# VectorE instead of GpSimd adds the probability blocks of a pair of heads in a transformer kernel

## The reference

```python
x = L0_attn_x                                              # (8, 512, 128)
x = x + _L0_attn_ref(_layernorm(x), Wq, Wk, Wv, g_scale)   # 16 heads of 8, cosine attention, no mask
x = x + _L0_ffn_ref(_layernorm(x), ...)                    # top-1 of 8 experts, hidden width 32
x = x + _L1_attn_ref(_layernorm(x), w_q, w_k, w_v, w_o)    # 16 heads of 64, causal
x = x + _L1_ffn_ref(_layernorm(x), ...)                    # top-2 of 8 experts, hidden width 512, norm
# the causal attention of the second layer:
a = jnp.einsum('nhtd,nhsd->nhts', q, k) / math.sqrt(q.shape[3])
a = jnp.where(causal_forbidden[None, None], -jnp.inf, a)
a = jax.nn.softmax(a, axis=3)
y = jnp.einsum('nhts,nhsd->nthd', a, v).reshape(a.shape[0], t, -1)
return y @ w_o
```

## Time and profile before

| what | value |
|---|---|
| runs | 1461.98, 1465.96, 1473.85 us, median 1465.96 |
| the profiled execution | 1452.33 us, span 1450.6 |
| TensorE busy | 1281.0 us, 88% |
| VectorE busy | 952.6 us, 66% |
| ScalarE busy | 858.0 us, 59% |
| GpSimd busy | 607.1 us, 42% |
| sum_blocks on GpSimd | 64 x 1824, 1323 and 742 ns (L806, L809, L812) |

### The profile page before, as it was taken

How to read it: one execution, slowest core, us unless ns; L and a number is a source line. 1 busy time by engine, 2 the same in 40 slices (tenths; PEclk the granted TensorE clock), 3 DMA queues, 4 the chain that set the end, 5 groups by cost and what they waited for, 6 DMA issues and landing times.

```text
span 1450.6 us, 28493 instructions
## 1 busy us (share of the span) xinstructions
PE 1281.0 (88%) x9302; PEld 790.0 (54%) x9302; DVE 952.6 (66%) x3308; ACT 858.0 (59%) x1679; POOL 607.1 (42%) x783
## 2 busy tenths in 40 slices
PE   3877899999999999999999999998888886989982
PEld 1223455555555555555555555555555554878872
DVE  4475665677677766767676776656665762776784
ACT  3766666676666766675666676654534542555563
POOL 1000133342444435442533453345435444657674
PEclk8979999999999999999999999999989998999996
DMA  8041290000000000000000000001010001142422
GB/s 339 1 187 71 9 5 1 1 9 1 8 9 16 8 2 16 8 9 1 23 2 8 7 11 1 8 9 66 8 73 16 1 8 41 53 115 70 129 65 92
DMA packets 65455, 54.68 MB, mean 38 GB/s; under 512 B 41016, under 2 KB 51648, under 8 KB 65056
## 3 DMA queue, kind: packets, MB, share of 16 engines
q1 hardware_dynamic: 60768, 43.48, 14.0%
q0 software_dynamic: 4544, 9.38, 1.9%
HBM read 21.03 MB, written 31.81 MB: 36 GB/s over the span
## 4 chain that ended last, share of the span: by engine, by line
PE 61%; DVE 17%; ACT 10%; issue 7%; POOL 2%; POOLq 1%; DMA 0%; ACTq 0%; SPq 0%; DVEq 0%
PE scores L1745 11%; PE outs L1763 9%; PE outs L1889 7%; PE work L1685 7%; PE work L1792 4%; DVE scores L1238 3%; PE scores L1876 3%; DVE ra L1231 3%; ACT a_buf L947 3%; ACT ra L953 3%; PE outs L1968 2%; PE scores L1714 2%; PE work L1692 2%; PE work L1851 1%; PE work L1802 1%
## 5 line engine op out<-in xcount | busy, mean ns | idle before, releaser
L1238 DVE CUSTOM_DVE_ANT_0 scores<-scores,mask_qk 128x512 f32<-128x512 f32 (+3 forms) x512 | 238.8, 518 | 148.7 <-PE scores L1714 148.7
L941 ACT ACTIVATE big<-scores 128x1024 f32<-128x1024 f32 (+1 forms) x192 | 169.8, 885 | 214.3 <-PE scores L1745 214.2
L786 POOL TENSOR_SCALAR_AFFINE_SELECT big<-big 128x256 f32<-128x256 f32 x256 | 101.6, 410 | 461.0 <-ACT big L941 436.3
L947 ACT ACTIVATE a_buf<-scores 128x1024 f32<-128x1024 f32 x256 | 248.0, 1028 | 44.1 <-PE scores L1876 43.9
L1745 PE MATMUL scores<-ra 64*128 64x512 f32 (+3 forms) x1536 | 184.1, 345 | 10.6 <-ACT a_buf L947 4.7
L806 POOL TENSOR_TENSOR big<-big 128x768 f32<-128x768 f32 x64 | 116.8, 1824 | 136.2 <-issue 53.3
L1763 PE MATMUL outs<-big 128*64 128x512 f32 (+3 forms) x1024 | 156.9, 450 | 0.0
L1745 PEld LDWEIGHTS scores<-ra 64*128 64x128 f32 x1536 | 121.5, 187 | 61.7 <-issue 41.5
L1231 DVE TENSOR_TENSOR ra<-work,ra 128x512 fp32r<-128x512 f32 x128 | 88.3, 690 | 89.4 <-ACT ra L953 89.4
L1889 PE MATMUL outs<-a_buf 128*16 128x512 f32 x1024 | 143.8, 637 | 1.5 <-ACT a_buf L947 1.4
L1022 ACT ACTIVATE big<-scores,b_sb 128x128 f32<-128x128 f32 x312 | 89.4, 370 | 76.2 <-PE scores L1956 75.2
(11 more groups left out here) (223 smaller groups left out, 2540.5 us busy)
## 6 DMA issues: line engine op xcount, KB each, us to landing
sorted_rows<-xrows SPq DMA_DIRECT2D x34, 520.0 KB, 6.9
qkT<-sorted_rows SPq DMA_DIRECT2D x78, 65.0 KB, 1.8
a_buf<-in_w SPq DMA_DIRECT2D x2, 2048.0 KB, 7.9
a_buf<-in_x SPq DMA_DIRECT2D x8, 256.0 KB, 2.7
x_rows<-x SPq DMA_DIRECT2D x8, 256.0 KB, 2.0
ra<-x_rows SPq DMA_DIRECT2D x8, 256.0 KB
a_buf<-choice_rows SPq DMA_DIRECT2D x6, 256.0 KB, 3.9
yT<-choice_rows SPq DMA_DIRECT2D x5, 256.0 KB, 2.7
```

The source lines that it names most:

```text
L941: activation(prob1(g, i), d[:, :, 0:256] if i == 2 else d, ACT.Exp, scale=SCALE1).then_inc(unit_free("pair", g, i), 1)
L947: activation(prob0(c)[:, i * 1024:(i + 1) * 1024], unit_wait(act, "cosine", c, i), ACT.Exp).then_inc(unit_free("cosine", c, i), 1)
L1238: return v.tensor_tensor_reduce(scores_, scores_, mask_qk[:, SEQ - width:SEQ], -1.0, 3e38, ALU.add, ALU.min, neg_max[:, qt, j:j + 1])
```

## The change

GpSimd keeps the four masks of a pair, the fourth where `sum_blocks` stood. The three additions go to VectorE, one step later: between the first and the second maxima of step g+1, behind whatever else VectorE does there. With them the waits that held them back and the semaphore `tsum_step` disappear. VectorE waits for the four masks of pair g and for the sum of pair g-1 before the first addition, and for its own result (`link`) before the second and the third. TensorE's `sums1` still waits for `tsum_ready`.

```diff
-            def sum_blocks(g, p, f, s, h):
-
-                causal(g, 2, 0)
-                if g + 1 < ALL_PAIRS:
-                    pool.wait_ge(negmax_ready, g + 2)
-                if p in (1, 3, 5) and s is not None:
-                    pool.wait_ge(parts_ready, s * GROUPS0 + p // 2 + 2)
...
-                pool.wait_ge(prob_masked, 4 * (g + 1))
-                nc.gpsimd.tensor_tensor(tsum, prob1(g, 0)[:, :, P:SEQ], prob1(g, 1)[:, :, 0:3 * P],
-                                        ALU.add).then_inc(tsum_step, 1)
...
                 if o.pair(0) is not None:
-                    sum_blocks(o.g, p, f, o.s, h)
+                    causal(o.g, 2, 0)
...
+            def sum_blocks(g):
+
+                if g:
+                    work_wait(dve, "sum", g - 1)
+                dve.wait_ge(prob_masked, 4 * (g + 1))
+                link(v.tensor_tensor(tsum, prob1(g, 0)[:, :, P:SEQ], prob1(g, 1)[:, :, 0:3 * P],
+                                     ALU.add))
+                link(v.tensor_tensor(tsum[:, :, P:3 * P], tsum[:, :, P:3 * P], prob1(g, 2),
+                                     ALU.add))
+                v.tensor_tensor(tsum[:, :, 2 * P:3 * P], tsum[:, :, 2 * P:3 * P],
+                                prob1(g, 1)[:, :, 3 * P:4 * P], ALU.add).then_inc(tsum_ready, 1)
...
                 if p == 7 and h is not None:
                     unit_rows(h)
+                if o.pair(-1) is not None:
+                    sum_blocks(o.pair(-1))
                 if o.pair(1) is not None:
                     maxima(o.pair(1), 1)
```

More of the change, by code:

```diff
@@ L519, in layers_kernel @@
         tsum_ready = sem("tsum_ready")
-        tsum_step = sem("tsum_step")
         rsum1_ready = sem("rsum1_ready")
```

## The result

The changed kernel takes **1510.6 us** (median of four runs, 1507.4 to 1512.2) against 1464.4 for the kernel before on the same chip: a ratio of 1.030, interval 1.027 to 1.033, so 46 us slower. The forecast was 1500 in a range of 1475 to 1518. Its side, its mechanism and most of its terms hold; the total came out 12 us short (46 against 34), and the experiments are about those 12 us.

What follows compares the result with a forecast made beforehand. TensorE bounds the kernel, waiting mainly for VectorE's maxima: 23 us in passes 0 to 4, 6 in the last three and 5 for the clock make 34, 1486 on the profiled execution, a median of 1500 us, range 1475 to 1518.

Steps and rivals of the forecast that it cites:

- Price of a set, 2.05 us: VectorE's three additions in one step, estimated at 0.96, 0.69 and 0.42 us; bounds 1.62 and 2.5 us.
- p=2, 4 and 5 nothing: Steps 2, 4 and 5 of a pass: VectorE's idle time or TensorE's later wait covers the additions, no cost.
- p=1 nothing: Step 1 of a pass: second maxima 0.65 us late, less 0.63 us of relief from GpSimd's additions, no cost.
- p=3 2.05, p=6 1.5, p=7 1.03: TensorE's loss in us in steps 3, 6 and 7 of a pass, waiting for VectorE's late maxima.
- Moving GpSimd's second_rows ahead, and its scatters, costs nothing: nobody waits for them: GpSimd's remaining work, started earlier: no cost, as nobody waits for it in the middle of the program.
- The clock, 5 us: TensorE's granted clock falls behind longer waits, every second pass or so, 1.5 us a fall; none to 12 us in all.
- Passes 5 to 7, 6 us: Last three passes, where streams end: 6 us together, mainly TensorE waiting for second maxima at p=5.
- TensorE swallows p=6 and 7: Rival: other waits make up the third maxima's lateness, only p=3 costs; +10, 1476 us; chance 0.12.
- Relief wins: Rival: VectorE's 4 us of relief a pass all lie on the path; faster, 1444 us; chance 0.04.
- Nothing is swallowed: Rival: 2.5 us a set, p=1 and p=5 pay too, a clock fall each pass; +57, 1523 us; chance 0.10.
- The additions stand still: Rival: VectorE's first addition blocked up to 5 us by a mask behind GpSimd's scatters; 1530 us; chance 0.02.
- The rule against the sum: VectorE and GpSimd share ports by exclusive lock; additions and masks would exclude each other, some 6 us more over five passes.

Runs made afterwards that it cites:

- e1_none: The changed kernel with no engine making the additions (constant ones instead, denominators not the reference's): 1458.9 us against 1461.3 before, ratio 0.998.
- e6_none_held: No additions on either engine, but GpSimd keeps the waits of the old sum_blocks: 1449.1 us, ratio 0.990 to the kernel before.
- e7_p3: VectorE makes the additions in step p=3 alone, GpSimd in all other steps: 1481.8 us, one run.
- e3_tight: VectorE adds only in steps p=3, 6 and 7, GpSimd with its waits in the others: 1488.5 us, ratio 1.017 to the kernel before.
- e5_after_held: The changed kernel, but GpSimd keeps the old sum_blocks waits behind the fourth mask: 1506.6 us, ratio 1.030 to the kernel before.
- e8_p3_one: VectorE's part of step p=3 alone, with only the first of its three additions, the other two left out: 1464.2 us, one run.
- the second profile: The kernel before, profiled once more with the same instructions on each engine: 1463.1 us, one run; profiled span 1461.3 against 1450.6 in the first.
- e2_both: GpSimd adds as before and VectorE repeats the same additions behind GpSimd's: 1532.2 us, ratio 1.048 to the kernel before.
- e4_calm: VectorE adds only in steps p=0, 1, 2, 4 and 5, GpSimd in the others: 1482.8 us, ratio 1.011 to the kernel before.
- e9_p3_behind: The changed kernel with step p=3's additions moved behind the second maxima: 1497.0 us, ratio 1.024 to the kernel before.
- e10_p3_behind_held: The changed kernel with step p=3's additions behind the second maxima and GpSimd's old waits kept: 1484.7 us, ratio 1.014 to the kernel before.

## Why the prediction was right, and where its sum was off

- **What bounds the kernel.** TensorE, with VectorE's maxima as the releaser that matters: held. GpSimd's additions off the path: held in the main. Without them the ratio is 0.998 (e1_none) and, with GpSimd's other work held in its place, 0.990 (e6_none_held); so they cost at most 1%, by slowing VectorE beside them.
- **Price of a set, 2.05 us:** measured 2.06. The wait on the masks cost nothing: there is no idle time before the first addition.
- **p=2, 4 and 5 nothing:** held within 0.1 us in passes 1, 2 and 4 (in pass 3 a fall of the clock of the kernel before is gone at p=5). **p=1 nothing:** it costs 0.41 to 0.48 in passes 1 to 4, and p=0 gives 0.65 and more back where the clock stays, with or without additions (e6_none_held too), as the first maxima of p=1 come earlier. Net nothing, as forecast, and for the reason given.
- **p=3 2.05, p=6 1.5, p=7 1.03:** 2.0 (e7_p3 less a fall), 1.41 to 1.54 where the clock stays, and 1.01 to 1.05 (e3_tight). These are the terms that were worked out from starts and idle times on both engines, and they are right to some hundredths.
- **"Moving GpSimd's second_rows ahead, and its scatters, costs nothing: nobody waits for them":** wrong. It is true that nobody waits for them, but `second_rows` slows VectorE while it runs beside it, and beside the scatters the step p=7 is longer: without additions on either engine the difference is 10 us. In the change itself p=3 doesn't show it (e5_after_held is as long there); p=7 does, 0.7 to 0.9 us in passes 1, 2 and 4. With the waits held passes 0 to 4 are 3.0 us shorter; the medians, 1506.6 and 1510.6, are too close to tell.
- **The clock, 5 us, "a fall in every second pass or so":** this is the term that was mis-sized. The price per fall was right (1.5 us forecast, 1.5 measured); the count wasn't. At p=3 it fell in each of the five passes, in three of them for 6.8 us. Time at the lower clock in passes 0 to 4 rose from 6.8 to 34.1 us; at 1.5 us for 3.4 that is 12 us, and with the last passes 21 us, where the forecast had 5 for the whole program (its upper bound of 12 is a fall in each of eight passes). The forecast took the earlier trace rows, one fall behind a wait of 1.16 us among five such waits, for a chance that holds for any wait; e8_p3_one and e7_p3 show that at p=3 it rises with the length of the wait, and a wait of 2.3 us had it each time. A pass was forecast at 142 us; passes 1 to 4 took 144.4, 144.8, 144.4 and 147.4.
- **Passes 5 to 7, 6 us:** measured 14.5. Time at the lower clock there rose by 20.5 us, worth 9 by the same price, which leaves 5.5 for the waits. That split is arithmetic, not an experiment, but TensorE's waits for maxima there did grow from 8.2 us (6.3 in the second profile) to 14.9. So the 6 us were right for the waits, and the rest is the clock again.
- **Not foreseen on the good side:** pass 0 gives back 3.3 us in its first three steps, with or without additions on VectorE. The sentence that the other whole passes repeat the idle times of pass 2 doesn't hold for pass 0 (3.17, 1.54 and 5.48 us at p=0 to 2, and 3.49 at p=5).

The sum with measured sizes, in us: 23 for the waits, 12 for the clock and 3 for the scatters in passes 0 to 4, less 4 of relief (3.3 in pass 0, 0.2 in each further one), is 34, where the two profiles of before give 33.7 and 31.7; with 14.5 for the last passes 48.5, where the medians give 46 and the ratio 44, within 40 and 48.5. So the side and the terms of the waits were reasoned right, and that 1510.6 lies inside the range is in part the width of the range: its upper end stood mainly on a dearer addition (2.5 us a set), which didn't come, and not on the many falls, which did.

**The rivals.** *TensorE swallows p=6 and 7* falls with e3_tight. *Relief wins* gets at best the 1% that e6_none_held shows, when nobody makes the additions. *Nothing is swallowed* came nearer on the clock (12 us, against 21 measured) and was wrong on the waits. *The additions stand still* never occurred.

**The rule against the sum.** By the Trainium skill, page "SBUF — State Buffer", section "SBUF: two separate sides", additions and masks would have locked each other out, for 6 us. VectorE's first addition kept its time (937 to 1191 ns, median 953), and so did the second (691 to 803, median 692); the third took 507 to 510 ns beside a mask and 424 without one. Of the masks the mean rose from 410 to 455 ns: the 47 of 256 that met an addition took 655 ns in the mean. So it was mostly GpSimd's operation that waited, and no such 6 us are in TensorE's waits. The stretched L1197, which the prediction took for a fit, is no case of two inputs (`mean<-mean`). The same rule does fit what the early `second_rows` did to an operation of VectorE with two inputs, 0.68 us instead of 0.19; it should have been asked of every operation that the change moves, not only of those that it adds.

## What to carry to other kernels

Before an operation moves to a less busy place on another engine, ask of that place what stands behind it: 2 us of work cost 3.3 to 4.6 us ahead of the maxima that TensorE waited for, and nothing behind them, 1.5 us later. Look on both engines at what moves up when a wait is deleted: sum_blocks' waits also held the work behind them, and without additions on either engine removing them cost 10 us. And where TensorE is nearly always busy, price a new wait of it at its length plus what the clock takes behind it: here 1.5 us a fall, in each pass behind the longest wait.

## What the runs showed of the hardware

- A wait of TensorE of 2.3 to 2.6 us in p=3 was followed by 3.4 or 6.8 us at a granted clock of 0.50 in all 25 cases (passes 0 to 4 of the change, e2_both, e3_tight, e5_after_held and e7_p3). A wait of 1.08 us at the same place was in 3 of 5 (e8_p3_one), a wait of 1.35 to 1.38 us in p=6 in 8 of 24 (the change, e3_tight, e5_after_held, e9_p3_behind, e10_p3_behind_held). Length alone doesn't decide: a wait of 0.81 us in p=3 had a fall in 8 of 12 (e1_none, e4_calm, e9_p3_behind). 3.4 us at that clock cost 1.4 to 1.5 us, 6.8 us about 2.4.
- A VectorE operation on 128x8 elements took 0.68 us beside GpSimd's addition of 128x512 (1.29 us) and 0.19 without it; eight operations on 128x64 took 1.59 us beside GpSimd's copy of 128x512 and 1.16 without it. GpSimd's addition was not longer for it (1.29, 1.27).
- Where an addition of VectorE and a mask of GpSimd overlapped, the addition of 128x512 kept its 0.69 us in passes 0 to 4 of the change, and the mask took up to 0.96 us instead of 0.41.
- While GpSimd issued its indirect transfers, the step p=7 was 0.7 to 0.9 us longer, with TensorE's wait for ScalarE at 1.24 us instead of 0.40 in pass 2, though neither engine needs GpSimd there. What they share was not tried.
